# Delta-rule attention kernel: the order of gate, value, joining and half-size products on TensorE in the loop

## The chip, the cores and the metric

The kernel runs on one core of one Trainium2 chip. The metric is the device time of one execution in microseconds, as the median of several runs.

## The reference, cut to what matters

The input x (2 sequences of 4096 tokens, 512 channels, f32) is normalized (xn), and the output is x + attention(xn) + ffn(xn). The attention is a chunkwise delta rule with 4 heads of 128 channels, to which a multi-scale convolution of v and a gate over three parts are added. What the change is about are two pieces:

```python
# delta rule, per chunk and head: the inverse of a unit lower triangle
attn = -jnp.einsum('bhncd,bhned->bhnce', kbc, kc) * strict_lower
for i in range(1, chunk):
    upd = jnp.einsum('...j,...ji->...i', attn[..., i, :], attn[..., :, :i])
    attn = attn.at[..., i, :i].add(upd)
attn = attn + jnp.eye(chunk)
...
# feed-forward part
r = jax.nn.sigmoid(jnp.einsum('btc,dc->btd', xr, W_r))          # "gate"
k_act = jnp.square(jax.nn.relu(jnp.einsum('btc,dc->btd', xk, W_k)))
out = r * jnp.einsum('btc,dc->btd', k_act, W_v)                 # "value"
```

## The kernel before, in words

The 4096 tokens of both sequences (here called batches, b = 0 and 1) are worked off in NS = 32 steps s of 128 tokens. The kernel takes a chunk of 128 tokens for the delta rule, so each step inverts 8 triangles of 128 x 128 (2 batches x 4 heads). All products are f32; each matmul of the program shows as two records in the trace, and the four heads or blocks of one product stand behind each other.

The inverse is built up by size. GpSimd inverts 16 x 16 blocks (`invert_units`), which go through DRAM into `Yq`. On TensorE, in the bank `cell[0]` (called `inv`), `inverse_W` and `inverse_Z` make 32 x 32 blocks of them, `join_W` and `join_Z` (lines 649, 661 and 663) make 64 x 64 blocks, and `half_W` and `half_X` (lines 672 and 680, products of 64 x 64) make the whole. Between them other engines copy:

- VectorE: `mask_W`, `step_Y` (line 1877) and `turn_Y` serve `inverse_Z` and `join_W`.
- ScalarE: `copy_W` (1263) serves `join_Z`; `spread_X` (1255, 1257) and `join_X` (1273, 1274) serve `half_W`; `copy_half_W` (1280) serves `half_X`; `join_half_X` (1285) serves `key_state(s, 0)` and the solves.

Behind the inverse come `key_state` (689, the keys times the state S), `subtract_state` on VectorE (1882, y less that product), `solve` (696, the inverse times y), `copy_u` on ScalarE (1295), `outputs` (703, 704) and `state` (710).

The feed-forward part has `ffn_key` (721), `gate_out` (734, bank `dense[0]`) and `value_out` (744, bank `dense[1]`). `gate_out(s, b, part)` and `value_out(s, b, part)` each do half of the four products of 128 x 128 by 128 x 512 that are summed in the bank: part 0 does the first two, part 1 the last two and signals `gate_mm` or `value_mm`. Their readers are `tanh_gate` (1346, ScalarE) and `gate_value` (1907, VectorE). Much of VectorE's time goes to `taps` (1924): single taps of the multi-scale convolution, which wait for little and stand between all else.

The order of the work is written out by hand, one list of calls for each engine. Each engine works through its list in order, and an engine waits where a call's semaphores are not there yet. The loop `for i in range(2, NS)` of TensorE's list (from line 908) has 30 passes; its last part works on step i - 1, which goes through steps 1 to 30. Steps 0 and 31 stand in lists of their own ahead of and behind the loop, which the change leaves alone. ScalarE's list for the same stretch of a step is: `relu_key` (1334) of the second pair, `copy_W`, `copy_mix`, `square_key`, `copy_tokens` and `sum_tokens` (1196, 1207), then in the next pass `spread_X`, `join_X`, `scale_v` (1246) twice, `copy_half_W`, `join_half_X`, `copy_u` twice, `tanh_gate`. VectorE's is: `step_Y`, five taps, `turn_Y`, 30 taps, `subtract_state(s, 1)`, six taps, `subtract_state(s, 0)`. (In the loop's last step ScalarE's list is another one: there `scale_v` and `shift` stand among the copies and `tanh_gate` ahead of `copy_half_W`.)

`join_Z` waits for `copy_W` and for the second `turn_Y`. `half_W` waits for `spread_X` and `join_X`. `half_X` waits for `copy_half_W`. `gate_out(s, 0, 0)` waits for the mixed input and for the first `relu_key`, `value_out(s, 0, 0)` for both `square_key`.

Of the kernel before, what the change touches and what calls it, by code (L numbers as in the profile page):

```python
# [74 lines left out]
def build(nc, x, out, w):  # L75
    NS = x.shape[1] // P
    with ExitStack() as ctx:
# [106 lines left out]
        def rows(r):  # L184
            return slice(r * Q, (r + 1) * Q)
# [4 lines left out]
        def hs(h):  # L190
            return slice(h * P, (h + 1) * P)
# [358 lines left out]
        def tensor_program(e):  # L550
# [44 lines left out]
            def turn_tokens(s, n):  # L595
                j, b = divmod(n, NB)
                e.wait_ge(*silu_done.upto(s, 3 - 2 * j))
                if n:
                    e.wait_ge(*tok_done.upto(s, n - 1))
                elif s:  # L600
                    e.wait_ge(*tok_done.upto(s - 1))
                for h in range(H):
                    t = kT[:, h, hs(b)] if j == 0 else vT[s % 2][:, h, b, VH:VH + P]
                    i = e.transpose(turn[:, hs(h)], t, ident)
                i.then_inc(tok_turned.sem, 1)
# [48 lines left out]
            def join_Z(s):  # L654
                e.wait_ge(*Y_turned.upto(s))
                e.wait_ge(*Wo_done.upto(s))
                for j in range(NB * H):
                    b, h = divmod(j, H)
                    z = slice(W + j * Q, W + (j + 1) * Q)
                    for r in (0, 2):  # L660
                        i = e.matmul(inv[rows(r), z], Wq[rows(r + 1), b, h, :], Xq[rows(r + 1), b, h, :],
                                     start=True, stop=True)
                    i = e.matmul(inv[rows(1), z], Xq[rows(1), b, h, :], Wq[rows(1), b, h, :], start=True, stop=True)
                i.then_inc(Z_mm.sem, 1)

            def half_W(s):

                e.wait_ge(*X_done.upto(s))
                e.wait_ge(*X_spread.upto(s))
                for j in range(NB * H):  # L670
                    b, h = divmod(j, H)
                    i = e.matmul(inv[HP:P, j * HP:(j + 1) * HP], Bm[0:HP, b, h * P + HP:(h + 1) * P], YW[0:HP, b, h, :],
                                 start=True, stop=True)
                i.then_inc(Wh_mm.sem, 1)
# [24 lines left out]
            def outputs(s, b):  # L699
                e.wait_ge(*u_done[b].upto(s))  # L700
                e.wait_ge(*aT_done.upto(s, b))
                for h in range(H):
                    e.matmul(cell[b][:, hs(h)], qT[:, h, hs(b)], S[:, b, hs(h)], start=True, stop=False)  # L703
                    i = e.matmul(cell[b][:, hs(h)], aT[:, b, hs(h)], u[:, b, hs(h)], start=False, stop=True)  # L704
                i.then_inc(o_mm.sem, 1)

            def state(s, b):
                e.wait_ge(*o_done.upto(s, b))
                for h in range(H):
                    i = e.matmul(cell[b][:, hs(h)], ktok[:, b, hs(h)], u[:, b, hs(h)], start=True, stop=True)  # L710
                i.then_inc(kTu_mm.sem, 1)
# [14 lines left out]
            def gate_out(s, b, part):  # L726
                if part == 0:
                    e.wait_ge(*mixed_in.upto(s))
                    if b == 0:
                        e.wait_ge(*key_relu.upto(s, 0))  # L730
                    else:
                        e.wait_ge(*gated.upto(s, 0))
                for k in range(2 * part, 2 * part + 2):
                    i = e.matmul(dense[0][:, :], xr[:, k, hs(b)], wr[:, k, :], start=(k == 0), stop=(k == CB - 1))  # L734
                if part == 1:
                    i.then_inc(gate_mm.sem, 1)

            def value_out(s, b, part):
                if part == 0:
                    e.wait_ge(*key_done.upto(s))  # L740
                    if b == 1:
                        e.wait_ge(*gated.upto(s, 0))
                for k in range(2 * part, 2 * part + 2):
                    i = e.matmul(dense[1][:, :], ka[:, k, hs(b)], wfv[:, k, :], start=(k == 0), stop=(k == CB - 1))  # L744
                if part == 1:
                    i.then_inc(value_mm.sem, 1)

            def kernel_mix(s, h):
                if s == 0:
                    e.wait_ge(mix_w_in, 16)  # L750
                e.wait_ge(*taps_done.upto(s, 3 * h + 2))
                if h:
                    e.wait_ge(*mix_done.upto(s, h - 1))
                elif s:
                    e.wait_ge(*l_bias.upto(s - 1))
                for p in range(3):
                    i = e.matmul(s_mix, km[:, p, :], my[h % 2][:, p, :], start=(p == 0), stop=(p == 2))  # L757
                i.then_inc(mix_mm.sem, 1)
# [14 lines left out]
            def turn_features(s):  # L773
                if s == 0:
                    e.wait_ge(scaled, N_SCALED)
                if s == NS - 1:
                    keep_streaming(s, 3)
                e.wait_ge(*f_low.upto(s))
                for b in range(NB):
                    e.matmul(s_ft[:, hs(b)], fparts[:, b, :, :, :].rearrange("p j i n -> p (j i n)"), ident16[:, :],  # L780
                             start=True, stop=True).then_inc(f_turned.sem, 1)
# [126 lines left out]
            for i in range(2, NS):  # L908
                kernel_mix(i - 2, 2)
                outputs(i - 2, 0)  # L910
                outputs(i - 2, 1)
                gate_out(i - 2, 1, 0)
                gate_out(i - 2, 1, 1)
                value_out(i - 2, 1, 0)
                value_out(i - 2, 1, 1)
                state(i - 2, 0)
                kernel_mix(i - 2, 3)
                state(i - 2, 1)
                channel_mix(i - 2, 0, 0)
                channel_mix(i - 2, 0, 1)  # L920
                channel_mix(i - 2, 1, 0)
                channel_mix(i - 2, 1, 1)
                project(i - 1, 5, 0)
                project(i - 1, 5, 1)
                turn_features(i - 2)
                hidden(i - 2, 0, 0)
                hidden(i - 2, 0, 1)
                hidden(i - 2, 1, 0)
                hidden(i - 2, 1, 1)
                turn_tokens(i - 1, 0)  # L930
                hidden(i - 2, 2, 0)
                hidden(i - 2, 2, 1)
                turn_tokens(i - 1, 1)
                hidden(i - 2, 3, 0)
                hidden(i - 2, 3, 1)
                logits(i - 2, 0)
                beta_and_q_norm(i - 1)
                logits(i - 2, 1)
                turn_tokens(i - 1, 2)
                turn_logits(i - 2)  # L940
                turn_beta(i - 1)
                kernel_mix(i - 1, 0)
                gram(i - 1, 0)
                gram(i - 1, 1)
                turn_x(i, 0)
                query_key(i - 1, 0)
                query_key(i - 1, 1)
                turn_x(i, 1)
                kernel_mix(i - 1, 1)
                key_state(i - 1, 1)  # L950
                project(i, 0, 0)
                project(i, 0, 1)
                project(i, 1, 0)
                project(i, 1, 1)
                project(i, 2, 0)
                project(i, 2, 1)
                project(i, 3, 0)
                project(i, 3, 1)
                turn_o(i - 2, 0)
                project(i, 4, 0)  # L960
                project(i, 4, 1)
                turn_o(i - 2, 1)
                attend(i - 2, 0, 0)
                attend(i - 2, 0, 1)
                attend(i - 2, 1, 0)
                attend(i - 2, 1, 1)
                ffn_key(i - 1, 0, 0)
                ffn_key(i - 1, 0, 1)
                inverse_W(i - 1)
                inverse_Z(i - 1)  # L970
                ffn_key(i - 1, 1, 0)
                ffn_key(i - 1, 1, 1)
                join_W(i - 1)
                turn_tokens(i - 1, 3)
                join_Z(i - 1)
                gate_out(i - 1, 0, 0)
                gate_out(i - 1, 0, 1)
                value_out(i - 1, 0, 0)
                value_out(i - 1, 0, 1)
                half_W(i - 1)  # L980
                half_X(i - 1)
                key_state(i - 1, 0)
                solve(i - 1, 1)
                solve(i - 1, 0)
# [1763 lines left out]
```

## Time and profile before

| what | us |
|---|---|
| median of 3 runs | 3519.88 |
| lowest and highest of them | 3506.42, 3535.21 |
| the profiled execution, its own time | 3516.6 |
| its span, first to last instruction | 3514.4 |
| TensorE busy (matmuls) | 3333.0 |
| VectorE busy | 3165.4 |
| ScalarE busy | 2758.5 |
| GpSimd busy | 823.5 |

The mean granted clock of TensorE over the span is 0.983 of its full speed. In the rows PE is TensorE's matmuls, DVE is VectorE, ACT is ScalarE. All times in rows are microseconds from the span's start, unless a row's head says otherwise.

### The profile page before, as it was taken

Reading aid. Unit: us, or ns where it says so; the run is one execution under the profiler, and the core shown is the slowest. Engines: PE = TensorE matmul, PEld = TensorE weight load, DVE = VectorE, ACT = ScalarE, POOL = GpSimd, SP = SyncE. Lnnn points to the kernel's source line nnn. Section 1 sums busy time; section 2 is a strip of 40 time slices with the busy share of each in tenths; the row PEclk is TensorE's granted clock in tenths of the full one; section 3 lists DMA queues with packets and bytes.
Section 4 is the critical chain, followed back from the end, with each engine's and each line's share of the span. In section 5 each row is a group of like instructions: output and inputs, shape, how many; then the busy total and the mean of one; then the engine's idle time right before and its main releaser. Section 6 shows DMA issues by size and latency. Waiting matters only on the chain.

```text
span 3514.4 us, 70437 instructions
## 1 busy us (share of the span) xinstructions
PE 3333.0 (95%) x22880; PEld 2459.5 (70%) x22880; DVE 3165.4 (90%) x7841; ACT 2758.5 (78%) x9146; POOL 823.5 (23%) x1501
## 2 busy tenths in 40 slices
PE   7999999999999999999999999999999999999988
PEld 5666777667776677766777767777766777667764
DVE  6998999999988998999989989998999889999994
ACT  5777888778787777877778877788777788777875
POOL 2322221122221222212222112222112222122211
PEclk9999999999999999999999999999999999999999
DMA  6022211122211222112222112221112221122211
GB/s 186 18 40 51 51 35 38 29 51 51 48 29 24 51 51 50 31 32 40 51 51 41 35 26 51 51 50 32 37 33 51 50 47 31 31 44 51 45 30 21
DMA packets 188310, 154.96 MB, mean 44 GB/s; under 512 B 111804, under 2 KB 146108, under 8 KB 187688
## 3 DMA queue, kind: packets, MB, share of 16 engines
q0 software_dynamic: 31744, 79.70, 13.1%
q1 hardware_dynamic: 156200, 70.76, 7.6%
q8 instruction: 183, 3.00, 0.3%
q14 instruction: 183, 1.50, 0.1%
HBM read 51.34 MB, written 52.95 MB: 30 GB/s over the span
## 4 chain that ended last, share of the span: by engine, by line
PE 35%; DVE 22%; ACT 21%; issue 10%; DMA 9%; POOL 3%; SPq 0%; ACTq 0%; DVEq 0%; POOLq 0%
DVE my L1924 16%; PE dense L811 7%; DMA my<-prod 5%; PE dense L734 5%; PE dense L744 5%; PE dense L721 4%; ACT my L1361 3%; PE small L757 2%; DMA rows_out<-Bm 2%; ACT dense L1394 2%; PE cell L703 2%; PE cell L704 2%; POOL Xu L464 1%; DMA Bu<-rows_out 1%; PE cell L696 1%
## 5 line engine op out<-in xcount | busy, mean ns | idle before, releaser
L1924 DVE SCALAR_TENSOR_TENSOR my<-vT,mw,my 128x256 f32<-128x256 f32 x5408 | 2257.1, 482 | 41.1 <-DMA my<-prod 22.3
L422 POOL TENSOR_SCALAR vare<-xsq 128x2 f32<-128x2 f32 x32 | 6.0, 187 | 2037.0 <-ACT xsh L1104 2037.0
L811 PE MATMUL dense<-xsh,w 128*128 128x256 f32 x2016 | 474.5, 381 | 3.8
L811 PEld LDWEIGHTS dense<-xsh,w 128*128 128x128 f32 x2016 | 362.6, 190 | 70.9 <-ACT xr L1426 10.9
L1334 ACT ACTIVATE ka<-dense 128x512 f32<-128x512 f32 x64 | 38.2, 596 | 313.6 <-PE dense L721 313.6
L721 PE MATMUL dense<-xk,wfk 128*128 128x256 f32 x1024 | 249.9, 400 | 11.6 <-DVE xb L1992 10.9
L721 PEld LDWEIGHTS dense<-xk,wfk 128*128 128x128 f32 x1024 | 199.3, 199 | 65.1 <-issue 37.1
L574 PE MATMUL front<-xsh,wq 128*128 128x256 f32 x1024 | 238.2, 386 | 0.6 <-ACT raw L1142 0.6
L734 PE MATMUL dense<-wr,xr 128*128 128x512 f32 x512 | 235.1, 602 | 0.0
L574 PE MATMUL front<-xsh,wv 128*128 128x256 f32 x1024 | 229.9, 382 | 2.7 <-ACT xsh L1119 2.7
L574 PE MATMUL front<-xsh,wk 128*128 128x256 f32 x1024 | 228.2, 379 | 3.8 <-ACT raw L1142 3.8
L744 PE MATMUL dense<-wfv,ka 128*128 128x512 f32 x512 | 230.2, 592 | 0.0
L1372 ACT ACTIVATE prod<-vT,mw 128x256 f32<-128x256 f32 x480 | 211.3, 515 | 23.1 <-DMA my<-prod 22.1
L482 POOL DMA_DIRECT2D my<-prod x160 | 146.3, 915 | 343.6 <-ACT my L1361 290.5
L848 PE MATMUL dense<-wo,ms 128*128 128x512 f32 x512 | 225.8, 593 | 0.0
L574 PEld LDWEIGHTS front<-xsh,wq 128*128 128x128 f32 x1024 | 196.2, 194 | 41.5 <-issue 14.8
L769 PE MATMUL dense<-cm,ym 128*128 128x512 f32 x512 | 225.0, 592 | 0.0
L574 PEld LDWEIGHTS front<-xsh,wk 128*128 128x128 f32 x1024 | 193.4, 189 | 33.6 <-ACT raw L1142 5.0
L574 PEld LDWEIGHTS front<-xsh,wv 128*128 128x128 f32 x1024 | 193.6, 192 | 29.8 <-ACT xsh L1119 2.3
L757 PE MATMUL small<-my,km 128*128 128x256 f32 x768 | 192.5, 387 | 1.4 <-DVE my L1924 1.0
L464 POOL TENSOR_TENSOR Xu<-Xu,Tu 64x28 f32<-64x28 f32 (+3 forms) x448 | 184.2, 411 | 35.1
L461 POOL TENSOR_TENSOR Tu<-Bu,Xu 64x28 f32<-64x28 f32 (+3 forms) x448 | 176.7, 394 | 30.4
(188 smaller groups left out, 6846.2 us busy)
## 6 DMA issues: line engine op xcount, KB each, us to landing
my<-prod POOLq DMA_DIRECT2D x160, 384.0 KB, 4.2
xa<-in_x SPq DMA_DIRECT2D x32, 512.0 KB, 4.4
rows_out<-Bm SPq DMA_DIRECT2D x64, 256.0 KB, 4.2
out<-xb POOLq DMA_DIRECT2D x32, 512.0 KB, 14.8
Yq<-units_out SPq DMA_DIRECT2D x128, 32.0 KB, 2.3
w<-in_w SPq DMA_DIRECT2D x1, 2048.0 KB, 16.2
Bu<-rows_out SPq DMA_DIRECT2D x32, 64.0 KB, 3.1
units_out<-Xu SPq DMA_DIRECT2D x32, 64.0 KB, 2.5
```

Source lines behind the costliest of these rows:

```text
L461: e.tensor_tensor(Tu[:, 0:n, 0:j + 1], Bu[:, j, j + 1:HQ][:, :, None].broadcast_to([UNITS, n, j + 1]), Xu[:, j, 0:j + 1][:, None, :].broad ...
L464: left = e.tensor_tensor(Xu[:, j + 1:HQ, 0:j + 1], Xu[:, j + 1:HQ, 0:j + 1], Tu[:, 0:n, 0:j + 1], ALU.subtract)
L574: i = e.matmul(by_batch(front[pair % 2][:, c * W:(c + 1) * W]), wt[:, k, hs(c0 + c)], xsh[s % 2][:, k, :, 1:1 + P], start=(k == 0), stop=( ...
L721: i = e.matmul(dense[pair][:, c * W:(c + 1) * W], wfk[:, k, hs(2 * pair + c)], xk[:, k, :], start=(k == 0), stop=(k == CB - 1))
L734: i = e.matmul(dense[0][:, :], xr[:, k, hs(b)], wr[:, k, :], start=(k == 0), stop=(k == CB - 1))
L744: i = e.matmul(dense[1][:, :], ka[:, k, hs(b)], wfv[:, k, :], start=(k == 0), stop=(k == CB - 1))
L757: i = e.matmul(s_mix, km[:, p, :], my[h % 2][:, p, :], start=(p == 0), stop=(p == 2))
L769: i = e.matmul(dense[b][:, :], ym[:, k, hs(b)], cm[:, k, :], start=(k == 0), stop=(k == CB - 1))
L811: e.matmul(by_batch(o), w1[:, k, hs(2 * pair + c)], xsh[s % 2][:, k, :, 1:1 + P], start=(k == 0), stop=False)
L848: i = e.matmul(dense[b][:, :], ms[:, b, hs(h)], wo[:, h, :], start=(h == 0), stop=(h == H - 1))
L1372: i = e.activation(by_batch(prod[:, p, :]), vT[s % 2][:, c, :, off:off + P], ACT.Copy, scale=mw[:, col:col + 1])
L1924: i = e.scalar_tensor_tensor(o, vT[s % 2][:, c, :, off:off + P], mw[:, col:col + 1], o, ALU.mult, ALU.add)
```

## The change

In the loop of TensorE's list two calls change places with their neighbours. The first half of `gate_out(i - 1, 0, .)` comes ahead of `join_Z` rather than behind it, and `half_W` comes between the two halves of `value_out(i - 1, 0, .)` rather than behind both. The banks are different ones (`dense[0]`, `dense[1]` and `cell[0]`), and every wait and signal stays with its call.

```diff
@@ -972,12 +972,12 @@
                 ffn_key(i - 1, 1, 1)
                 join_W(i - 1)
                 turn_tokens(i - 1, 3)
+                gate_out(i - 1, 0, 0)
                 join_Z(i - 1)
-                gate_out(i - 1, 0, 0)
                 gate_out(i - 1, 0, 1)
                 value_out(i - 1, 0, 0)
+                half_W(i - 1)
                 value_out(i - 1, 0, 1)
-                half_W(i - 1)
                 half_X(i - 1)
                 key_state(i - 1, 0)
                 solve(i - 1, 1)
```

## Rows read from the trace of the kernel before

**Rows 1.** The page: span, busy time by engine, shares of the chain.

```profile
span 3514.4 us, 70437 instructions
...
PE 3333.0 (95%) x22880; PEld 2459.5 (70%) x22880; DVE 3165.4 (90%) x7841; ACT 2758.5 (78%) x9146; POOL 823.5 (23%) x1501
...
PE 35%; DVE 22%; ACT 21%; issue 10%; DMA 9%; POOL 3%; SPq 0%; ACTq 0%; DVEq 0%; POOLq 0%
```

**Rows 2.** Timeline of TensorE, one pass: start, duration, line, tiles, count, [idle before].

```profile
1616.29 0.69 PE L649 MATMUL cell<-Yq,Bm 32*32 32x32 f32 x32
1616.91 0.66 PE L604 MATMUL turn<-cst,vT 128*128 128x128 f32 x4
1617.56 0.22 PE L661 MATMUL cell<-Xq,Wq 32*32 32x32 f32 x2
...
1618.19 3.70 PE L734 MATMUL dense<-wr,xr 128*128 128x512 f32 x8
1621.73 3.60 PE L744 MATMUL dense<-wfv,ka 128*128 128x512 f32 x8
1625.25 1.14 PE L672 MATMUL cell<-YW,Bm 64*64 64x64 f32 x16
1627.08 1.14 PE L680 MATMUL cell<-X,YW 64*64 64x64 f32 x16 [0.68 <-ACT YW L1280]
1628.89 1.16 PE L689 MATMUL cell<-S,kT 128*128 128x128 f32 x8 [0.67 <-ACT X L1285]
```

**Rows 3.** Timeline of ScalarE, the same pass.

```profile
1616.40 0.60 ACT L1334 ACTIVATE ka<-dense 128x512 f32<-128x512 f32 x1 [1.90 <-PE dense L721]
...
1619.83 1.63 ACT L1255 COPY X<-Xq 32x256 f32<-32x256 f32 x4
...
1623.06 0.36 ACT L1274 COPY YW<-cell 32x256 f32<-32x256 f32 x1
1623.45 2.45 ACT L1246 ACTIVATE y<-vtok,nrm 128x128 f32<-128x128 f32 x8
1626.43 0.59 ACT L1280 ACTIVATE YW<-cell 64x512 f32<-64x512 f32 x1 [0.54 <-PE cell L672]
```

**Rows 4.** Timeline of VectorE, the same pass.

```profile
1612.77 0.29 DVE L1877 TENSOR_TENSOR Yq<-Yq,cell 128x128 f32<-128x128 f32 x1
...
1615.44 11.92 DVE L1924 SCALAR_TENSOR_TENSOR my<-vT,mw,my 128x256 f32<-128x256 f32 x30
...
1627.88 2.45 DVE L1924 SCALAR_TENSOR_TENSOR my<-vT,mw,my 128x256 f32<-128x256 f32 x6
1630.26 0.67 DVE L1882 TENSOR_TENSOR y<-y,cell 128x512 f32<-128x512 f32 x1
```

**Rows 5.** The list of waits: us in total, times, longest.

```profile
PE cell L680 <- ACT YW L1280: 22.7, 32, 1.4
...
DVE y L1882 <- PE cell L689: 18.6, 15, 2.4
```

**Rows 6.** Stretches from 3 us after half_W: length, PE busy, granted clock, DMA.

```profile
224.72:228.72 4.00, 3.37 (x17) 0.57 0.00 0
...
1628.25:1632.25 4.00, 3.31 (x26) 1.00 0.00 0
...
2804.64:2808.64 4.00, 3.37 (x16) 0.59 0.00 0
```

**Rows 7.** The 11 passes with a clock fall there, half_W to half_W.

```profile
1518.61:1625.25 106.64, 103.23 (x715) 0.98 0.21 42
...
sum 1189.52, PE 1143.32; mean PE 103.94
```

**Rows 8.** The 18 other passes, half_W to half_W.

```profile
1625.25:1730.70 105.45, 102.05 (x715) 1.00 0.21 42
...
1946.54:2054.43 107.89, 103.79 (x715) 0.98 0.21 42
...
sum 1921.20, PE 1848.73; mean PE 102.71
```

## The prediction, on record before the changed kernel was run

> **What bounds the kernel now.** I read the page first. TensorE is busy for 3333.0 of 3514.4 us (95%) and VectorE for 90%, yet the chain that ended last gives TensorE only 35%, VectorE 22% and ScalarE 21% [rows 1]. So no engine bounds alone: the work goes from one to the next, and a microsecond saved on TensorE counts only where TensorE is the one that the others wait for. The next view was the order in time of one loop pass, engine by engine. I took the pass whose half_W begins at 1625.25 us. The reader is to see three things in it.
>
> First, TensorE runs join_W, the token turn and join_Z in some 1.9 us, then all eight gate records and all eight value records without a pause (3.5 us each), and then comes the thin stretch: half_W 1.14 us, a wait of 0.68 us for ScalarE's copy, half_X 1.14 us, a wait of 0.67 us for the next copy, key_state [rows 2]. Second, ScalarE has no pause from 1616.40 to the end of scale_v at 1623.45 + 2.45 = 1625.90; join_X (the copies that half_W needs) is over at 1623.06 + 0.36 = 1623.42, some 1.8 us before half_W asks for it, and copy_half_W then waits 0.54 us for TensorE [rows 3]. Third, VectorE runs from step_Y at 1612.77 through 30 and 6 taps to subtract_state(0) at 1630.26 with no idle shown [rows 4], while key_state ended at 1628.89 + 1.16 = 1630.05 [rows 2]. In this pass solve(0) therefore waits for VectorE, not for the half-size products.
>
> The third view is the list of waits: TensorE waited before half_X 32 times, 22.7 us in all, and VectorE waited for key_state 15 times, 18.6 us in all [rows 5]. So roughly half of the passes are paced by VectorE at this place and half by TensorE.
>
> The fourth view is the granted clock, in stretches of 4 us that begin 3 us after half_W. In 11 of the 30 loop passes it is 0.50 to 0.66 there, in the other 19 it is 1.00 [rows 6]: just behind the thin stretch TensorE falls from its 2.4 to its 1.2 GHz level. What it did before each of those falls was half_W, the wait, half_X, the wait and the first key_state products. I then measured each whole pass from one half_W to the next. The 11 passes with such a fall take 1189.52 us, 108.14 each [rows 7]; the 18 others take 1921.20 us, 106.73 each, and the undisturbed ones among them some 105.45 [rows 8].
>
> **The change, part by part.** No instruction is added or removed, on any engine; only TensorE's order differs, in the 30 passes of the loop. No DMA is issued by TensorE and no queue is passed by the move.
>
> *First half of gate_out(0) ahead of join_Z.* It is four records of 3.54/8 = 0.44 us, so join_Z comes 1.8 us later, at about 1617.56 + 1.8 = 1619.3 [rows 2]. Who waits for join_Z? Only join_X on ScalarE, which comes up in its own order at 1619.83 + 1.63 + 0.85 = 1622.31, behind spread_X [rows 3]. join_Z is done at about 1619.95, so 2.3 us of cover are left; cost nothing. If ScalarE's token sums were absent the join would cost up to 1.8 us a pass. The gate itself ends where it did (its consumer, ScalarE's tanh, runs behind copy_u). The gate needs nothing that join_Z makes. The value of this half of the edit on its own is nothing here: the stretch join_W, turn, join_Z is 1.9 us of small work, and no fall followed it in this trace.
>
> *half_W between the value halves.* TensorE now reaches half_W after join_W, the turn, gate, join_Z and half of value: 1625.25 less 4 x 0.44 = 1623.5. Its input is there at 1623.42 [rows 3]. So it fits to within 0.1 us, and a wait of up to 0.1 us may show there. Then four value records (1.75 us) run while ScalarE works. half_W ends at 1624.65, scale_v at 1625.90, so copy_half_W no longer waits for TensorE but for its own engine; it ends at 1625.90 + 0.59 = 1626.49. TensorE's second value half ends at 1624.65 + 1.75 = 1626.4, or 1626.5 with 0.1 us for the switch of tile shape (the change from value to half_W shows less than 0.1 us). half_X can start at about 1626.55 instead of 1627.08: 0.5 us earlier, with its wait down from 0.68 to 0.15 or less. The wait behind half_X (0.67) stays.
>
> What are these 0.5 us worth? In a pass paced by VectorE nothing, since subtract_state(0) starts at 1630.26 either way, and TensorE waits 0.5 us there instead. Of the 15 waits of VectorE for key_state [rows 5], 11 are the passes with a clock fall, which stand in the next term. 4 remain: 4 x 0.5 = 2 us. Bounds: 0 and 30 x 0.68 = 20 us.
>
> *The clock behind it.* This is the term that decides. The thin stretch from half_W to key_state was 1628.89 - 1625.25 = 3.64 us long with 2.28 us of work in 64-row products, and 1.35 us of waits. After the change 1.75 us of full-size products stand in the middle, and what is left in one piece is half_X, a wait of 0.67 us and key_state, about 1.8 us before full-height products are back. The trace shows that pieces of small products of 1.9 us (join_W to join_Z) are borne without a fall. So I take it that the 11 falls go. The price of one: 108.14 - 106.73 = 1.41 us a pass [rows 7, 8], 15.5 us for 11. Bounds: 0 if the falls stay, and 11 x (108.14 - 105.45) = 29.6 us if those passes become undisturbed ones. I take 15.5, since passes without this fall still have others: 6 of the 18 are below 1.00 in granted clock, as the one of 107.89 us at 0.98 [rows 8], most of them at the quarter-size products of inverse_Z, where this change moves nothing.
>
> A rule of the Trainium skill speaks against this term: the page "TensorE: Matmul & The Clock Gate", section "HAM oscillation — how this bites in real kernels", has the clock fall after long pauses of TensorE, as behind a wait for DMA. By that rule pauses of 0.7 us could not lower it, and the sum would be the 2 us alone. The rows disagree: the clock fell here in 11 passes and the longest pause before any of these falls was 0.7 us [rows 2, 6]. I go by the rows.
>
> *Other edges.* value_mm(0) comes 1.2 us later; its reader gate_value(0) is some ten microseconds behind on VectorE. In the last loop pass ScalarE has another order; I count nothing for it.
>
> **Sum.** 15.5 + 2 = 17.5 us. The profiled execution took 3516.6 us (span 3514.4 and 2.2 around it), which gives 3499.1. The median of the runs is 3519.88, 3.3 us above; for a median I go to 3502, -0.5%. About 1% (35 us) is what a measurement of this kernel can tell from no change, its three runs being 29 us apart.
>
> **The rivals.**
>
> *A. The falls stay (0.18).* The thin work is still thin: half_X, wait, key_state follow one another, and the value half may only shift the place. For it: ScalarE's copies still stop TensorE once. Against it: the longest thin piece is halved. Time: only 2 to 7 us (up to 15 passes x 0.5), 3513 to 3518.
>
> *B. The falls go and others go with them (0.15).* If TensorE, no longer late, also meets the inverse better, the passes come near to 105.45: 29 x (107.27 - 105.45) = 53 us, where 107.27 is (1189.52 + 1921.20)/29 [rows 7, 8]. Fully so 3463 to 3467; partly 3475. Against it: the six falls in the other passes had nothing to do with half_W.
>
> *C. The clock falls at inverse_Z instead (0.17).* Passes then are all paced by VectorE, and TensorE, ahead, waits longer at inverse_Z for VectorE's mask_W (22.5 us over 32 now). One such fall costs 107.89 - 105.45 = 2.4 us or more [rows 8]. It decides from 17.5/2.4 = 7 more falls on: with 10 more the time is 3502 + 24 = 3526, above the time before. To be slower by over 1% it would have to happen in some 22 more of 30 passes, 3555. For it: all four such falls in passes without a fall at half_W came where VectorE paced. Against it: most passes so paced had none.
>
> *D. The order gives back what it wins:* half_W waits for join_X by more than I find, as ScalarE's row is full. Each 0.1 us costs nothing until half_X is later than before, 0.5 us; it would then look like A.
>
> **How the numbers follow.** My forecast (0.50) is 3502, its own range 3490 to 3512. A has 0.18, B 0.15, C 0.17 (D within A). The range 3478 to 3525 takes in A, most of C's near end and the part of B in which only some other falls go. Faster by over 1% (under 3485) is B and the lower edge of the forecast with luck: 0.18. Slower by over 1% is the far end of C: 0.04. Within 1%: 0.78.
>
> **What would show it.** Right: granted clock 1.00 in the 4 us behind 3 us after half_W in nearly all passes; the wait before half_X under 0.2 us a pass instead of 0.7; copy_half_W with no idle ahead of it; TensorE's wait for VectorE before solve(0) up to 0.5 us in undisturbed passes; passes of 105.4 us more frequent, none shorter by much. Wrong: falls at the same place in 8 or more passes (A), more passes with a wait at inverse_Z and a low clock behind it (C), or half_W waiting over 0.3 us for ScalarE (D).

## The result, and the profile of the changed kernel

The changed kernel takes 3491.08 us in the median of 7 runs (3480.96 to 3496.58), the kernel before 3514.99 us in the median of 7 (3506.42 to 3535.21). The ratio is 0.9927, with a 95% interval of 0.9905 to 0.9949: 0.73% faster, some 26 us. The profiled execution took 3488.17 us, its span is 3485.9 us, some 28 us less than before [rows 1], and the mean granted clock is 0.991 where it was 0.983.

The page of the changed kernel: span, busy times, shares of the chain.

```profile
span 3485.9 us, 70437 instructions
...
PE 3314.3 (95%) x22880; PEld 2429.7 (70%) x22880; DVE 3162.7 (91%) x7841; ACT 2760.5 (79%) x9146; POOL 824.9 (24%) x1501
...
DVE 30%; PE 27%; ACT 20%; issue 10%; DMA 9%; POOL 3%; SPq 0%; ACTq 0%; DVEq 0%; POOLq 0%
```

The instructions are the same in number, yet TensorE's busy time fell by 19 us: the same products ran at the full clock more of the time. And the chain has changed its leader. VectorE was 22% of it and TensorE 35% [rows 1]; now it is 30% and 27%.

By a fall I mean a stretch in which the granted clock drops to the 1.2 GHz level, and by an undisturbed pass one without a fall. TensorE's timeline of one undisturbed pass of the changed kernel (columns as in [rows 2]), and then ScalarE's and VectorE's for the same pass:

```profile
2235.08 0.69 PE L649 MATMUL cell<-Yq,Bm 32*32 32x32 f32 x32
...
2236.20 1.88 PE L734 MATMUL dense<-wr,xr 128*128 128x512 f32 x4
...
2238.64 1.98 PE L734 MATMUL dense<-wr,xr 128*128 128x512 f32 x4
2240.46 1.88 PE L744 MATMUL dense<-wfv,ka 128*128 128x512 f32 x4
2242.27 1.14 PE L672 MATMUL cell<-YW,Bm 64*64 64x64 f32 x16
2243.34 1.98 PE L744 MATMUL dense<-wfv,ka 128*128 128x512 f32 x4
2245.35 1.14 PE L680 MATMUL cell<-X,YW 64*64 64x64 f32 x16
2247.16 1.16 PE L689 MATMUL cell<-S,kT 128*128 128x128 f32 x8 [0.67 <-ACT X L1285]
2248.16 1.06 PE L696 MATMUL cell<-y,X 128*128 128x128 f32 x8
2249.78 1.16 PE L696 MATMUL cell<-y,X 128*128 128x128 f32 x8 [0.56 <-DVE y L1882]
```

```profile
2241.85 0.36 ACT L1274 COPY YW<-cell 32x256 f32<-32x256 f32 x1
2242.24 2.45 ACT L1246 ACTIVATE y<-vtok,nrm 128x128 f32<-128x128 f32 x8
2244.71 0.59 ACT L1280 ACTIVATE YW<-cell 64x512 f32<-64x512 f32 x1
```

```profile
2249.04 0.68 DVE L1882 TENSOR_TENSOR y<-y,cell 128x512 f32<-128x512 f32 x1
```

Count from the start of join_W (line 649), which is the same place in both orders. half_X began 1627.08 - 1616.29 = 10.79 us behind it before [rows 2] and begins 2245.35 - 2235.08 = 10.27 us behind it now: 0.52 us earlier, and the row has no wait in brackets any more. half_W starts 0.06 us after join_X's last copy ends (2241.85 + 0.36 = 2242.21), so it fits just in time, as worked out. ScalarE's copy at line 1280 follows its own scale_v with no wait. Then comes the row that answers to the prediction's point on VectorE: the second half of the solves (line 696) waits 0.56 us for subtract_state(0), which starts at 2249.04. In the pass before the change it started 1630.26 - 1616.29 = 13.97 us behind join_W [rows 2, 4], here 13.96. The half microsecond is won on TensorE and given back 4 us later.

The granted clock in stretches of 4 us placed as in [rows 6] (1.2 us behind half_X's start), the first, that of the pass above, and the last of 30:

```profile
222.08:226.08 4.00, 2.83 (x23) 1.00 0.00 0
...
2246.55:2250.55 4.00, 2.83 (x23) 1.00 0.02 4
...
3304.72:3308.72 4.00, 3.39 (x27) 1.00 0.01 2
```

All 30 rows show 1.00; before it was 19 of 30. The passes from half_W to half_W, among them the three whose clock is below 1.00, and the sum over 29:

```profile
217.80:329.86 112.06, 104.23 (x716) 0.97 0.20 40
...
965.67:1074.44 108.77, 103.82 (x716) 0.98 0.20 41
...
1814.83:1923.40 108.57, 103.89 (x715) 0.98 0.20 41
...
2242.27:2347.70 105.43, 102.19 (x715) 1.00 0.21 42
...
sum 3082.73, PE 2970.56; mean PE 102.43
```

The same 29 passes took 1189.52 + 1921.20 = 3110.72 us before [rows 7, 8]. So 28.0 us came out of the passes, nearly all of what the two traces differ by. The usual undisturbed pass is the same, 105.43 against 105.45 us [rows 8]. What changed is how many passes are disturbed: 17 of 29 had a clock below 1.00 before, at 108.36 us in the mean, and 3 of 29 have it now. The passes at 1.00 did not get shorter in the mean: the 12 before have 105.71 us, the 26 now 105.90.

The falls behind half_W are only one kind among the 17. Three passes of the kernel before with a fall there, the first two with a second fall near inverse_Z:

```profile
546.03:655.19 109.16, 104.84 (x716) 0.97 0.20 41
975.42:1085.20 109.78, 105.42 (x715) 0.97 0.20 41
2054.43:2161.42 106.99, 103.35 (x715) 0.98 0.21 42
```

Sorted so, the trace before has 8 passes with the fall behind half_W alone (107.22 us in the mean), 3 with both (110.59), 4 with one near inverse_Z alone (108.36), 2 with one elsewhere (109.59) and 12 with none (105.71). The changed kernel's has 2 with one near inverse_Z, 1 with one elsewhere and 26 with none. A fall behind half_W thus costs 107.22 - 105.71 = 1.5 us, and 11 of them some 16.6 us. The other 11.4 of the 28.0 us are not from there: nine falls at other places became three, less 5 us by which the 26 passes are longer.

### The profile page after: what moved, and what is told of

Read it like the earlier page. It is cut to its first block, busy times and chain, and to the rows that moved or that the text cites. A ratio compares the mean times of both kernels' runs of the same rounds, so it can differ in the third digit from the quotient of the medians.

```text
span 3485.9 us, 70437 instructions
## 1 busy us (share of the span) xinstructions
PE 3314.3 (95%) x22880; PEld 2429.7 (70%) x22880; DVE 3162.7 (91%) x7841; ACT 2760.5 (79%) x9146; POOL 824.9 (24%) x1501
## 4 chain that ended last, share of the span: by engine, by line
DVE 30%; PE 27%; ACT 20%; issue 10%; DMA 9%; POOL 3%; SPq 0%; ACTq 0%; DVEq 0%; POOLq 0%
DVE my L1924 24%; PE dense L811 7%; DMA my<-prod 5%; PE dense L744 3%; PE dense L734 3%; ACT my L1361 3%; PE small L757 2%; ACT dense L1394 2%; PE cell L703 2%; PE dense L721 2%; DMA rows_out<-Bm 2%; PE cell L704 2%; POOL Tu L461 1%; POOL Xu L464 1%; DMA Bu<-rows_out 1%
## 5 line engine op out<-in xcount | busy, mean ns | idle before, releaser
L721 PE MATMUL dense<-xk,wfk 128*128 128x256 f32 x1024 | 239.7, 388 | 11.9 <-DVE xb L1992 11.7
L744 PE MATMUL dense<-wfv,ka 128*128 128x512 f32 x512 | 238.2, 598 | 0.0
L721 PEld LDWEIGHTS dense<-xk,wfk 128*128 128x128 f32 x1024 | 192.0, 192 | 62.0 <-issue 37.0
```

The source lines that it names most:

```text
L721: i = e.matmul(dense[pair][:, c * W:(c + 1) * W], wfk[:, k, hs(2 * pair + c)], xk[:, k, :], start=(k == 0), stop=(k == CB - 1))
```

## The experiments

The theory: full-size products between half_W and half_X keep TensorE at its 2.4 GHz level, and that, not the shorter wait, is the gain. Rivals: the gain is the 0.5 us by which half_X comes earlier; the gain is in the other edit, the split of gate and join_Z; any work in the pause, large or small, keeps the clock up. The ratios below are to the kernel before, run on the same chip. Falls are counted in the 30 loop passes, in the 4 us stretches of the last section; falls "near inverse_Z" in passes 1 to 29.

**One edit alone, and the other alone.**

```diff
 value_out(i - 1, 0, 0)
+half_W(i - 1)
 value_out(i - 1, 0, 1)
-half_W(i - 1)
 half_X(i - 1)
```

> half_W between the value halves, the gate and join_Z as before. Theory 1 (the full-size products between half_W and half_X keep TensorE's clock up): no fall behind half_W in the 30 loop passes, time as with the whole change, ratio to before 0.993 (0.990 to 0.996). join_Z is now done 1.8 us earlier, which no one needs; but half_W comes at the same time, so it still meets join_X within 0.1 us. Rival (the split of gate and join_Z carries part of the gain): a ratio between 0.995 and 1.000.

Measured: 3490.93 us, ratio 0.9931 (0.9904 to 0.9957), no fall behind half_W.

```diff
+gate_out(i - 1, 0, 0)
 join_Z(i - 1)
-gate_out(i - 1, 0, 0)
 gate_out(i - 1, 0, 1)
```

> First gate half ahead of join_Z, half_W and half_X one behind the other as before. Theory 1: falls behind half_W in 8 to 15 of 30 passes, ratio 0.998 to 1.002. Rival (the gate split matters, by breaking up the stretch join_W, turn, join_Z): ratio 0.997 or less.

Measured: 3515.02 us, ratio 1.0001 (0.9981 to 1.0021), 11 falls behind half_W. So the whole gain hangs on half_W's place, and moving the first gate half ahead of join_Z does nothing that can be measured, as worked out.

**The clock apart from the wait.** These two leave the order as before and put work that nobody reads into the pause behind half_W, into the bank `turn`, which is free there. They compute all that the kernel before does, and the fill besides.

```diff
 half_W(i - 1)
+fill_full(i - 1, 1)    # matmul(turn[:, :], ident, wfv[:, 0, :])
 half_X(i - 1)
```

> Order as before, but one extra product of 128x128 by 128x512 (two records, 0.86 us), whose result nobody reads, stands between half_W and half_X, in all loop passes. It covers the wait of 0.68 us and makes half_X about 0.2 to 0.3 us later than before. Theory 1 (clock): falls behind half_W in 0 to 2 passes and a ratio of 0.993 to 0.997, although half_X is not a bit earlier. Rival (the gain is the 0.5 us by which half_X comes earlier): ratio 1.000 to 1.003.

```diff
 half_W(i - 1)
+fill_small(i - 1, 6)   # matmul(turn[HP:P, 0:HP], cst[0:HP, 0:HP], wfv[0:HP, 0, 0:HP])
 half_X(i - 1)
```

> As the run with the extra full-size product, but with 6 extra products of 64x64 (12 records of 71 ns, 0.85 us), whose result nobody reads: the pause ahead of half_X is covered for as long, with small products. If what matters is how much of the array works: falls behind half_W remain in 4 to 12 of 30 passes, and a ratio of 0.998 to 1.003. Rival (pauses of TensorE lower the clock, small products do as well as big ones): no falls, and a ratio as with the full-size one.

TensorE's timeline in a pass without a fall behind half_W, first with the full-size fill, then with the small one (the fill is line 679; the added lines move the later line numbers):

```profile
1608.26 1.14 PE L672 MATMUL cell<-YW,Bm 64*64 64x64 f32 x16
1609.33 1.12 PE L679 MATMUL turn<-wfv,cst 128*128 128x512 f32 x2
1610.38 1.14 PE L685 MATMUL cell<-X,YW 64*64 64x64 f32 x16
```

```profile
1937.59 1.14 PE L672 MATMUL cell<-YW,Bm 64*64 64x64 f32 x16
1938.57 0.86 PE L679 MATMUL turn<-wfv,cst 64*64 64x64 f32 x12
1939.41 1.14 PE L685 MATMUL cell<-X,YW 64*64 64x64 f32 x16
```

With the full-size fill half_X starts 2.12 us behind half_W, 0.29 us later than the 1.83 of [rows 2]. With the small fill it starts 1.82 us behind it, where it always did, and there is no pause in front of it at all. The 0.67 us pause behind half_X stands in both, as in [rows 2]. Measured, full-size: 3496.11 us, ratio 0.9949 (0.9930 to 0.9967), no fall behind half_W. Small: 3510.58 us, ratio 0.9988 (0.9968 to 1.0009), 8 falls. The granted clock of one stretch of the run with the small fill, TensorE's row for half_X (line 685 in that run) in the same pass, which shows no wait, and the sum over its 29 passes:

```profile
1294.30:1298.30 4.00, 3.38 (x17) 0.57 0.00 2
```

```profile
1293.10 1.14 PE L685 MATMUL cell<-X,YW 64*64 64x64 f32 x16
```

```profile
sum 3106.95, PE 3007.90; mean PE 103.72
```

The pass sum with the full-size fill:

```profile
sum 3091.66, PE 2996.21; mean PE 103.32
```

This separates the causes at this place. Full-size work alone, with half_X later than ever, gives 3110.72 - 3091.66 = 19.1 us in the passes, 68% of the 28.0 (some of it, as in the changed kernel, from fewer falls elsewhere: 4 in this trace). Filling the pause for as long with 64-row products gives 3.8 us and leaves 8 falls, the one shown in a pass in which TensorE had no pause ahead of half_X. The intervals of the two ratios do not touch. So it is not the pause ahead of half_X that brings the fall, but the size of the products there, that is, how much of the array works. The 9 us between the run with the full-size fill and the changed kernel hold the fill's own 0.86 us a pass and the earlier half_X; these two I did not separate.

**Is the undisturbed pass paced by VectorE's subtraction?**

```diff
+subtract_state(i - 2, 0)
 taps(i - 2, 3, 42, 43)
 taps(i - 2, 3, 37, 38)
-subtract_state(i - 2, 0)
```

> The changed kernel, with VectorE's subtract_state(s, 0) two taps (0.8 us) earlier in its list. Now TensorE waits 0.56 us for it in nearly every pass. If VectorE's place of this one subtraction paces the pass (what the prediction said of undisturbed passes): half a microsecond less a pass, undisturbed passes of 104.9 instead of 105.45, ratio to before 0.988 to 0.991. Rival (the pace is set elsewhere, by VectorE's whole row or another wait, and TensorE gives the 0.5 us back in the next wait for it): ratio 0.992 to 0.994, as without it.

> The kernel before, with the same move of subtract_state(s, 0). There key_state ends 0.2 us ahead of the subtraction in undisturbed passes, and behind it in the others. Expected: at most 0.2 us in half of the passes, ratio 0.998 to 1.001, falls behind half_W in 8 to 15 passes. The two edits then gain together what neither gains alone.

Measured: on the changed kernel 3503.73 us, ratio 0.9965 (0.9941 to 0.9989); on the kernel before 3530.91 us, ratio 1.0034 (1.0013 to 1.0054), 13 falls behind half_W. Both are slower than without the move, on neither side of what I had expected. TensorE's timeline in the first of them shows where the half microsecond goes, at kernel_mix(3) (line 757), 13 us behind the solves:

```profile
2272.98 1.56 PE L757 MATMUL small<-my,km 128*128 128x256 f32 x6 [0.62 <-DVE my L1924]
```

Its list of waits, the row for the same wait over the whole run:

```profile
PE small L757 <- DVE my L1924: 19.1, 30, 1.0
```

The solves no longer wait, and kernel_mix(3) waits 0.62 us for the last of VectorE's taps instead. The pace is VectorE's whole row of taps up to kernel_mix(3), not the place of one subtraction in it; that was the rival, and it is right. Why it became slower: two taps that were apart now follow each other on the same sum (the rows start 0.51 us apart instead of 0.40), and this trace had 7 falls near inverse_Z against 2 in the changed kernel's. The first is 0.1 us a pass, out of the 0.26 by which the usual undisturbed pass is longer (105.69 against 105.43); whether the second comes from the move was not tried.

On the kernel before there is a further cause, and a larger one. The subtraction now stands ahead of the end of key_state, and VectorE, which paces, stops for it:

```profile
DVE y L1882 <- PE cell L689: 35.3, 30, 2.7
```

It was 18.6 us in 15 waits [rows 5]. The usual undisturbed pass of that run is 106.2 us, not 105.45.

**The same treatment at the quarter-size products of inverse_W and inverse_Z.** In the changed kernel TensorE still waited for VectorE between inverse_W and inverse_Z, in each pass. Its list of waits:

```profile
PE cell L640 <- DVE Wq L1872: 19.7, 31, 1.3
PE cell L696 <- DVE y L1882: 17.3, 28, 1.8
```

```diff
 inverse_W(i - 1)
-inverse_Z(i - 1)
 ffn_key(i - 1, 1, 0)
+inverse_Z(i - 1)
...
-step_Y(i - 2)
 taps(i - 2, 3, 9, 10)
 taps(i - 2, 2, 34, 35)
 taps(i - 2, 2, 53, 54)
+step_Y(i - 2)
```

> The changed kernel, and the same treatment for the quarter-size products: ffn_key(1, 0) (full-size, 1.8 us) stands between inverse_W and inverse_Z, and VectorE's step_Y three taps later. If full-size products in the midst of small ones keep the clock up wherever they are: the falls near inverse_Z (1 or 2 a trace in the changed kernel, 7 of 30 before) are gone, and TensorE's wait of 0.5 us a pass for mask_W is covered; ratio 0.987 to 0.991. Rival: the wait moves to another place (join_W for step_Y), ratio 0.992 to 0.996.

> Both further edits on the changed kernel. If their gains add: ratio 0.982 to 0.988. If both only hand the wait on to VectorE: 0.991 to 0.994.

Measured: 3482.20 us, ratio 0.9900 (0.9873 to 0.9927), and with the early subtraction besides 3490.14 us, ratio 0.9920 (0.9892 to 0.9947). The list of waits of the first:

```profile
DVE Yq L1877 <- PE cell L640: 12.7, 23, 3.2
...
PE cell L640 <- DVE Wq L1872: 1.9, 2, 1.4
```

TensorE's wait for mask_W is gone (19.7 to 1.9 us), but inverse_Z comes later, and step_Y on VectorE waited for it in 23 passes. Since VectorE is what paces, that is a loss, and the undisturbed pass is 105.67 us, longer than the 105.43 of the changed kernel; the gain is in the falls, of which one was left in 29 passes. This edit puts full-size work there and covers a wait at once, and no run separates the two at this place. The early subtraction made it worse again. So I moved step_Y one tap further, and ran beside it the changed kernel again, and the edit with three taps on the kernel before.

```diff
 taps(i - 2, 2, 53, 54)
-step_Y(i - 2)
 taps(i - 2, 3, 5, 6)
+step_Y(i - 2)
```

> The changed kernel with ffn_key(1, 0) between inverse_W and inverse_Z, and step_Y four taps later instead of three. With three, VectorE waited 0.3 us for inverse_Z in 23 passes, and its row was late by as much; with four that wait should be gone, and undisturbed passes go from 105.67 to 105.4 us. Expected: ratio 0.987 to 0.990, under the changed kernel's by 0.003 to 0.005. Rival (turn_Y right behind step_Y makes the same wait): as with three taps, 0.990.

> The changed kernel as it is, on the same chip as the next two, so that they can be held against it. Expected: ratio 0.991 to 0.995, no fall behind half_W.

> The kernel before (half_W and half_X one behind the other), with ffn_key(1, 0) between inverse_W and inverse_Z and step_Y three taps later. If the falls at the two places are separate: none near inverse_Z in steps 2 to 29, still 8 to 15 behind half_W, ratio 0.995 to 0.999. If the falls behind half_W bring on those at inverse_Z, and not the other way, the same. Rival (the clock is saved as well by either edit, so one suffices): falls behind half_W under 5, ratio 0.993 or less.

Measured: with four taps 3466.28 us, ratio 0.9849 (0.9825 to 0.9874); the changed kernel 3489.69 us, ratio 0.9924 (0.9900 to 0.9948), no fall behind half_W; the edit with three taps on the kernel before 3495.91 us, ratio 0.9936 (0.9914 to 0.9958), still 11 falls behind half_W and 2 near inverse_Z. TensorE's and VectorE's timelines of the version with four taps, then its list of waits, then one pass and the sum of 29:

```profile
2211.87 0.73 PE L629 MATMUL cell<-Yq,Bm 32*32 32x16 f32 x64
2212.52 1.99 PE L721 MATMUL dense<-xk,wfk 128*128 128x256 f32 x8
2214.45 0.73 PE L640 MATMUL cell<-Wq,Xq 32*32 32x16 f32 x64
```

```profile
2212.86 2.45 DVE L1924 SCALAR_TENSOR_TENSOR my<-vT,mw,my 128x256 f32<-128x256 f32 x6
2215.23 0.28 DVE L1877 TENSOR_TENSOR Yq<-Yq,cell 128x128 f32<-128x128 f32 x1
```

```profile
DVE Yq L1877 <- PE cell L640: 7.5, 5, 4.0
```

```profile
2224.22:2329.29 105.07, 102.33 (x715) 1.00 0.21 43
...
sum 3065.93, PE 2972.45; mean PE 102.50
```

In this pass neither engine waits at this place, the usual undisturbed pass is down from 105.43 to 105.07 us, and the version beats both kernels: 1.5% under the kernel before and 0.7% under the changed one, with intervals that do not touch. It gained more than I had expected, as did the edit on the kernel before, which I had put at 0.995 to 0.999.

The run on the kernel before shows one direction: the cure at inverse_Z leaves the 11 falls at half_W as they were. The gains still do not add. half_W's move alone is worth 1 - 0.9927 = 0.0073, the edit at inverse_Z with three taps alone 0.0064, and both together 0.0100. With the falls at inverse_Z already down to 2 and 1 in a trace, half_W's move is worth 0.9936 - 0.9900 = 0.0036, some 13 us, about half of what it is worth alone. The two ratios are from different chips and each is known to 0.002 or 0.003, so the 13 us are rough; but they agree with the 16.6 us of 11 falls, and not with the whole 26.

## Why the prediction was right, and which term was off

*Which views decide, and what bounds.* Right: undisturbed passes were VectorE's (105.45 and 105.43 us), and the gain is in the disturbed ones.

*First gate half ahead of join_Z: nothing.* Right, shown by itself (1.0001).

*half_X 0.5 us earlier.* Right: 0.52 us. half_W in time to within 0.1 us, the copy without a wait, the solves waiting "0.5 us there instead": each is a row above. Two readings under it were wrong. I wrote that in the pass of [rows 2] solve(0) waits for VectorE already. The whole trace before has only two such waits of TensorE, 1.3 us in all; in that pass their row shows no stop. And of VectorE's 15 waits for key_state not 11 but 9 stand in passes with a fall behind half_W, so that 6 were left, not 4. The 2 us that I gave this step would have been 3, and either can't be told from nothing.

```profile
PE cell L696 <- DVE y L1882: 1.3, 2, 0.9
```

*The 11 falls go.* Right: 0 in both traces of the changed kernel, in the run with half_W's move alone and in the one with the full-size fill.

*The price of one fall.* Right in size, with luck. I took 108.14 - 106.73 = 1.41 us, 15.5 us for 11. Both groups of passes were mixed: 3 of the 11 have a second fall near inverse_Z, and 6 of the 18 a fall somewhere. These two errors nearly cancelled. Like against like, 8 passes with this fall alone against 12 with none, it is 1.5 us and 16.6 for 11.

*The falls elsewhere: the term that was off.* I counted none of them as cured, since "this change moves nothing" at inverse_Z. The passes gave 28.0 us against my 17.5, and 11.4 of them are this term: 7 falls near inverse_Z and 2 elsewhere before, 2 and 1 in the changed kernel. It is the partial form of rival B, to which I had given 0.15. The time came out in my own range of 3490 to 3512 only by a microsecond, at 3491.08.

*Rivals.* A (the falls stay) fell with the first view. B (others go too) was half right. Near inverse_Z the trace before has 7 falls, the runs that kept the old half_W order without a cure 9, 7 and 6. The changed kernel has 2 and 4 in its two traces, half_W's move alone 5, the full-size fill 3, but the changed kernel with the early subtraction 7. That is fewer on the whole, and no run shows why. The traces show where they fall. TensorE's row for inverse_Z, first in a pass of the kernel before, with a fall right behind it, then in one of the changed kernel, with none:

```profile
2039.48 0.72 PE L640 MATMUL cell<-Wq,Xq 32*32 32x16 f32 x64 [1.20 <-DVE Wq L1872]
```

```profile
529.54 0.72 PE L640 MATMUL cell<-Wq,Xq 32*32 32x16 f32 x64 [1.34 <-DVE Wq L1872]
```

In the trace before each of the 7 passes in which TensorE stopped for 1.0 us or more between the start of inverse_W and the end of inverse_Z has a fall there, and no other pass has. In the changed kernel's trace there are again 7 such passes, and only 2 falls. So the stops did not become fewer, but fewer of them brought a fall. Why stays open, chance included, since each count is of one execution. C (more falls at inverse_Z) did not come. D fell: half_W waits only in the last loop pass.

*The skill's rule.* The Trainium skill's page "TensorE: Matmul & The Clock Gate", section "HAM oscillation — how this bites in real kernels", makes long pauses the cause of a fall; by it the sum was 2 us. The runs decide against it for this place: with the pause filled by small products the clock still fell in 8 passes, and with a full-size product in none. The same page, section "What's actually happening", has the clock set by how busy TensorE has been of late; the traces agree with that only if small tiles count for little. At inverse_Z, where the falls stand at stops of 1.0 us or more, no run separates pause and size.

## What to carry to other kernels

Look at the granted clock just behind stretches of small-tile products, pass by pass, also where TensorE shows 95% busy and there is no pause over 0.7 us. Put a full-size product between two small ones whose result another engine has to copy: it hides the copy and keeps the clock, and here nearly all of the worth was in the second. Price a fall against passes that have none at all, not against the rest, and count each place of falls by itself before you add. When an engine has got ahead of the one that paces, the next wait takes back what a reorder wins, so move the signals of the pacing engine with it, as step_Y was, but not to where that engine has to wait itself, as the early subtraction did on the kernel before.

## What the runs showed of the hardware that I had not expected

Products of 64 x 64 did not keep TensorE's clock up, even issued without a gap: 8 falls to the 1.2 GHz level in 30 passes, each behind about 3 us of them and the 0.67 us pause that follows. With one full-size product in their midst there was none. A fall behind half_W cost 1.5 us of a pass of 105.7 in the trace before, one near inverse_Z 108.36 - 105.71 = 2.65.

In bursts of 32-row products TensorE at times stopped for no other engine. In the changed kernel:

```profile
1803.88 0.17 PE L640 MATMUL cell<-Wq,Xq 32*32 32x16 f32 x1 [1.22 <-issue]
```

In the first loop pass such a stop was 3.9 us before and 4.2 us after the change, and in both that pass has a fall near inverse_Z. The profile names no releaser; I did not look for the cause.
